# Turning every third job's probabilities by DMA instead of TensorE, and three low halves on GpSimd

## The chip, the cores and the metric

The kernel runs on one core of one Trainium2 chip. The metric is the device time of one execution in microseconds. Beside it stands one profiled execution, from which all rows below are taken.

## The reference, cut to what matters

Input x is (4, 1024, 1024) in fp32, the context the same. The output is `x1 + ffn(layernorm(x1))` with `x1 = x + attention(layernorm(x), ctx, ctx)`:

```python
q, k, v = ...            # 16 heads of 64; k = v = context
scores = jnp.einsum('bhqd,bhkd->bhqk', q, kj) * SCALE
scores = jnp.where(causal, -jnp.inf, scores)      # key index > query index
p = softmax(scores); out = jnp.einsum('bhqk,bhkd->bhqd', p, v)
...
soft = sigmoid(pweight) - sigmoid(nweight)        # (1024, 1024, 4 bits)
weight = jnp.einsum('oin,n->oi', soft, exps * sigmoid(mask_weight)) * scale[0]
return jnp.einsum('bsi,oi->bso', input, weight) + bias
```

## The kernel before, in words

**Tiles and jobs.** The 4 x 1024 rows are 32 tiles of 128 queries; tile t has i = t % 8 and sees i + 1 blocks of 128 keys. The 16 heads of a tile are worked off in jobs of 4, 4, 2, 2, 1, 1, 1, 1 heads for i = 0 to 7, so a tile has 4, 8 or 16 steps, one job each; j.q is the step's number within its tile, j.n its number in the whole (352 in all). Tiles with i of 4 to 7 (16 steps, one head per job, 5 to 8 blocks) are called long here.

**Precision.** Every operand of a matrix product is held as two f16 numbers, a high half (ScalarE rounds) and a low half (what is left, by a subtraction), side by side. Scores are two products per key block (`qt`, and `qs`, which is `qt` with its two 64-row halves swapped by DMA).

**One job's way.** `scores` (TensorE, L354, L355, mask L358) into one of two `slot` banks; `maxima` (VectorE, L554); `exponentials` (ScalarE, L451) into `p32`; `transpose_p` (TensorE, L367) turns each fp32 block of `p32` into `ptb`, in pieces of up to four blocks; `high_parts` (ScalarE, L461) and `low_parts` (VectorE, L561) split each piece out of `ptb` into `pt_hi` and `pt_lo`; `values` (TensorE, L381, L383) multiplies them with the context into `oacc`. `output` (ScalarE, L468) copies four heads' results out, `add_attention` (GpSimd, L743 to L752) adds them to the tile's row.

**Order.** Each engine's program is a loop over the jobs, written out by hand, with semaphores between the engines. TensorE's step for job j is:

```python
scores(JOBS[j.n + 2])
values(JOBS[j.n - 2])
transpose_p(j)
linear(k, m0, m1)        # a share of the linear layer of tile k = t - 3 (L399)
```

ScalarE's is `output` of the group that job j-2 closed, `high_parts(j)`, `exponentials(j+2)`, then at fixed steps the high half of y (`y_split`, L490), of a context tile (`c_split`, L483) or of the queries (`q_split`, L475). VectorE's is `maxima(j+2)`, `reciprocals`, `low_parts(j)`, then at fixed steps the low halves of the same three (L601, L596, L590), the moments for the layer norms (L575, L578), and `result` (L610), which adds the linear layer's bank `ffnb` to the row and frees that bank. GpSimd computes the layer norms (`deviation`, `normalise` L719), `add_attention` and `add_bias` (L737).

**The DMA queue of SyncE (SP)** works in order too: in step 0 of a tile it stores tile t-4 and swaps `qs` of tile t+1; in the middle it loads x and the context of tile t+3; after y's low half it turns y (L283); in the last step it turns the keys (L264) and the queries (L270) of tile t+2. The turns are `dma_start_transpose`, which transposes f16 blocks of 128x128 from SBUF to SBUF. The fixed steps stand in the tables Y_HI, Y_LO, C_HI, C_LO, Q_STEPS and BIAS. In the first 16 steps, tiles 0 to 3, the weights are built beside the attention.

Of the kernel before, what the change touches and what calls it, by code (L numbers as in the profile page):

```python
# [6 lines left out]
ALU = mybir.AluOpType  # L7
# [6 lines left out]
P = 128  # L14
# [29 lines left out]
class Job:  # L44


    def __init__(self, n, t, q, chunk0):
# [6 lines left out]
        blocks = self.heads * (self.i + 1)  # L54
        count = -(-blocks // 4)
        size = -(-blocks // count)
# [7 lines left out]
for _t in range(TILES):  # L64
    FIRST.append(len(JOBS))
    for _q in range(H // HPJ[_t % NT]):
        JOBS.append(Job(len(JOBS), _t, _q, JOBS[-1].chunks[-1][0] + 1 if JOBS else 0))
FIRST.append(len(JOBS))
LAST_OF_GROUP = [j.n for j in JOBS if j.closes_group]
# [46 lines left out]
Q_STEPS = {4: (0, 1, 2, 3), 8: (1, 2, 4, 6), 16: (3, 5, 8, 11)}  # L116
BIAS = {4: 2, 8: 4, 16: 9}
# [25 lines left out]

def reached(eng, s, value):
    if value > 0:
        eng.wait_ge(s, value)


def build(nc, x, ctx_in, pweight, nweight, exps, bexps, mask_weight, scale, pbias, nbias, biasscale, out):
# [6 lines left out]
    with ExitStack() as stack:  # L156
# [10 lines left out]
        spare32 = sb("spare32", [P, DM], F32)  # L167
# [4 lines left out]
        qs = sb("qs", [P, 2, H, P], F16)  # L172
        p32 = sb("p32", [P, 2, 8 * P], F32)
        pt_hi = sb("pt_hi", [P, 2, 8 * P], F16)
        pt_lo = sb("pt_lo", [P, 2, 8 * P], F16)
# [20 lines left out]
        def as_f32(m, place):  # L196
# [4 lines left out]
                 (ring[:, 6, :], spare32[:, :]), (as_f32(v16, 5), as_f32(yt, 0))]  # L201
# [22 lines left out]
        t_done, hi_done, lo_done, pv_done = sem("t_done"), sem("hi_done"), sem("lo_done"), sem("pv_done")  # L224
        osb_done, osb_added = sem("osb_done"), sem("osb_added")
# [15 lines left out]
        def _(sp):  # L241
# [30 lines left out]
            def swap_q(t):  # L272
                sp.wait_ge(q_in[t % 2], 16 * (t // 2 + 1))
                sp.dma_start(qs[0:D, t % 2], qt[D:P, t % 2]).then_inc(qs_in[t % 2], 16)
                sp.dma_start(qs[D:P, t % 2], qt[0:D, t % 2]).then_inc(qs_in[t % 2], 16)
# [20 lines left out]
            swap_q(0)  # L296
# [9 lines left out]
            for t in range(TILES):  # L306
                n = steps(t)
                for s in range(n):
                    if s == 0:
                        if t >= 4:  # L310
                            store(t - 4)
                        if t + 1 < TILES:
                            swap_q(t + 1)
# [11 lines left out]
                    if s == n - 1 and t + 2 < TILES:  # L325
                        turn_k(t + 2)
# [11 lines left out]
        def _(pe):  # L338
            def scores(j):
                i, t = j.i, j.t  # L340
                reached(pe, p_done, j.n - 1)
                if j.q == 0:
                    pe.wait_ge(qs_in[t % 2], 32 * (t // 2 + 1))
                    pe.wait_ge(k_in[t % 2], 16 * (t // 2 + 1))
                place0 = t - i
                for hh in range(j.heads):
                    h, base = j.head0 + hh, hh * HEAD_STRIDE[i]
                    first = 0
                    while first <= i:
# [5 lines left out]
                        last = pe.matmul(dst, qs[:, t % 2, h, :], keys, start=False, stop=end <= i,  # L355
# [6 lines left out]
            def transpose_p(j):  # L362
                pe.wait_ge(p_done, j.n + 1)
# [7 lines left out]
            def values(j):  # L371
                if j.opens_group:
                    reached(pe, osb_done, j.group)
                pe.wait_ge(lo_done, j.chunks[-1][0] + 1)
                for hh in range(j.heads):
                    h = j.head0 + hh
                    for blk in range(j.i + 1):
                        k = hh * (j.i + 1) + blk
                        cols = slice(k * P, (k + 1) * P)
                        v = v16[:, (j.t - j.i + blk) % V_PLACES, h]  # L380
                        pe.matmul(oacc[:, h % GROUP, :], pt_hi[:, j.par, cols], v,  # L381
                                  start=blk == 0, stop=False, skip_group_check=True)
                        last = pe.matmul(oacc[:, h % GROUP, 0:D], pt_lo[:, j.par, cols], v[:, 0:D],  # L383
# [62 lines left out]
        def _(act):  # L446
            def exponentials(j):
                act.wait_ge(mx_ready, j.n + 1)
                for hh in range(j.heads):
# [5 lines left out]
                last.then_inc(p_done, 1)  # L455

            def high_parts(j):
                reached(act, pv_done, j.n - 1)
                for c, blocks in j.chunks:
                    act.wait_ge(t_done, c + 1)  # L460
                    nc.scalar.activation(pt_hi[:, j.par, P * blocks.start:P * blocks.stop],  # L461
                                         ptb[:, c % 2, 0:P * len(blocks)], ACT.Copy, scale=P_SCALE
                                         ).then_inc(hi_done, 1)
# [86 lines left out]
        def _(dve):  # L550
# [6 lines left out]
            def low_parts(j):  # L557
                for c, blocks in j.chunks:
                    dve.wait_ge(hi_done, c + 1)
                    cols = slice(P * blocks.start, P * blocks.stop)  # L560
# [261 lines left out]
```

## Time and profile before

| | us |
|---|---|
| median of 3 runs | 1275.42 (1273.55 to 1277.51) |
| profiled execution, its own time | 1274.72 |
| its span, first to last instruction | 1272.9 |
| TensorE busy (matmul) | 1166.4 (92%) |
| VectorE busy | 1034.5 (81%) |
| ScalarE busy | 928.5 (73%) |
| GpSimd busy | 597.1 (47%) |
| DMA queue q1, share of 16 engines | 47.2% |

The span is what the engines' records cover; the execution's own time is 1.8 us longer. A busy TensorE is not one at its peak, since matmuls overlap: its pace is read from the start of one group to the start of the next, as the chain of waits gives it. A wait is idle time of one engine with the instruction that ended it.

### The profile page before, as it was taken

What the parts mean: (1) busy time and instruction counts of PE and PEld (TensorE: products, weight loads), DVE (VectorE), ACT (ScalarE), POOL (GpSimd) and SP (SyncE); (2) the same over time, 40 slices, a digit from 0 to 9 for tenths busy, and PEclk for the clock granted to TensorE, in tenths of its full rate; (3) what the DMA queues carried; (4) which work ended last, traced back from release to release, by engine and by line L of the source; (5) the groups of instructions that cost most, each with busy time, mean ns of one, the idle gap of its engine ahead of it and who ended that gap; (6) DMA issues with size and microseconds to landing.
All of it is one profiled execution on the core that took longest, in us unless ns stands there. A gap on an engine that the chain in (4) does not pass through costs nothing.

```text
span 1272.9 us, 29189 instructions
## 1 busy us (share of the span) xinstructions
PE 1166.4 (92%) x11376; PEld 883.3 (69%) x11376; DVE 1034.5 (81%) x1593; ACT 928.5 (73%) x2019; POOL 597.1 (47%) x717
## 2 busy tenths in 40 slices
PE   0677788999999999999999999999999999999998
PEld 0666675677777677777776677787786677777763
DVE  4576677888898888888897888888988888888872
ACT  2688876777877777787777777777787787777750
POOL 3399865433324954433325853333237844332241
PEclk9888899999999999999999999999999999999999
DMA  8979843543224955433316764444326755220112
GB/s 220 305 242 309 296 133 80 127 98 79 68 84 82 203 133 123 90 90 70 97 51 138 166 144 102 103 82 100 67 68 150 169 131 117 67 68 19 35 34 66
DMA packets 228984, 152.92 MB, mean 120 GB/s; under 512 B 204272, under 2 KB 204272, under 8 KB 228848
## 3 DMA queue, kind: packets, MB, share of 16 engines
q1 hardware_dynamic: 227264, 148.92, 47.2%
q8 instruction: 91, 1.49, 0.5%
q10 hardware_dynamic: 1584, 2.14, 0.5%
q14 instruction: 45, 0.37, 0.1%
HBM read 67.15 MB, written 16.78 MB: 66 GB/s over the span
## 4 chain that ended last, share of the span: by engine, by line
PE 63%; DVE 15%; POOL 6%; issue 5%; ACT 5%; DMA 4%; SPq 2%; ACTq 1%; POOLq 0%
PE ffnb L399 19%; PE ptb L367 15%; PE oacc L381 7%; PE slot L354 7%; PE slot L355 7%; DVE pt_lo L561 5%; PE oacc L383 4%; DVE stats L575 4%; POOL v L758 3%; ACT pt_hi L461 2%; DVE mx L554 2%; PE slot L358 2%; DVE ring L610 1%; ACT osb L468 1%; DMA yt<-in_L_ffn_nweight_dram 1%
## 5 line engine op out<-in xcount | busy, mean ns | idle before, releaser
L561 DVE SCALAR_TENSOR_TENSOR pt_lo<-ptb,pt_hi 128x384 f16<-128x384 f32 (+2 forms) x688 | 382.8, 597 | 119.7 <-ACT pt_hi L461 117.5
L461 ACT ACTIVATE pt_hi<-ptb 128x384 f16<-128x384 f32 (+2 forms) x688 | 326.4, 527 | 166.2 <-PE ptb L367 165.5
L451 ACT ACTIVATE p<-slot,mx 128x512 f32<-128x512 f32 (+7 forms) x512 | 378.5, 748 | 52.1 <-DVE mx L554 50.0
L399 PE MATMUL ffnb<-wt,yt 128*128 128x512 f16 x1464 | 371.0, 379 | 19.7 <-DVE ring L610 17.9
L554 DVE TENSOR_REDUCE mx<-slot 128x1 f32<-128x640 f32 (+7 forms) x352 | 359.4, 1021 | 21.3 <-PE slot L358 18.6
L367 PE MATMUL ptb<-id,p 128*128 128x128 f32 x2304 | 323.7, 279 | 11.1 <-DVE pt_lo L561 10.0
L354 PE MATMUL slot<-kt,qt 128*128 128x128 f16 (+3 forms) x1056 | 270.5, 286 | 32.6 <-DMA qs<-qt 28.0
L743 POOL TENSOR_TENSOR att<-osb 128x256 f32<-128x256 f32 x128 | 99.1, 774 | 421.9 <-ACT osb L468 397.7
L355 PE MATMUL slot<-kt,qs 128*128 128x128 f16 (+3 forms) x1056 | 270.0, 285 | 0.0
L367 PEld LDWEIGHTS ptb<-id,p 128*128 128x128 f32 x2304 | 246.3, 141 | 18.2 <-issue 15.7
L381 PE MATMUL oacc<-v,pt_hi 128*128 128x128 f16 x2304 | 244.2, 220 | 3.6 <-DVE pt_lo L561 1.9
L383 PE MATMUL oacc<-v,pt_lo 128*128 128x64 f16 x2304 | 234.7, 193 | 0.0
L399 PEld LDWEIGHTS ffnb<-wt,yt 128*128 128x128 f16 x1464 | 140.8, 98 | 124.8 <-issue 23.9
L381 PEld LDWEIGHTS oacc<-v,pt_hi 128*128 128x128 f16 x2304 | 205.6, 98 | 20.2 <-ACT osb L468 2.6
L383 PEld LDWEIGHTS oacc<-v,pt_lo 128*128 128x128 f16 x2304 | 200.8, 98 | 0.4
L354 PEld LDWEIGHTS slot<-kt,qt 128*128 128x128 f16 x1056 | 105.8, 100 | 94.7 <-issue 33.9
L355 PEld LDWEIGHTS slot<-kt,qs 128*128 128x128 f16 x1056 | 104.6, 99 | 58.1 <-issue 0.6
L468 ACT ACTIVATE osb<-oacc 128x512 f32<-128x512 f32 x128 | 76.6, 599 | 53.5 <-PE oacc L383 52.7
L358 PE MATMUL slot<-maskb,idb 128*128 128x128 bf16 x512 | 112.0, 223 | 0.0
L451 ACT ACTIVATION_READ_ACCUMULATOR p<-slot,mx 128x1 f32 x512 | 108.5, 212 | 0.0
L752 POOL TENSOR_TENSOR ring<-ring,att 128x256 f32<-128x256 f32 x128 | 99.9, 781 | 10.1
L746 POOL TENSOR_TENSOR att<-att,rinv 128x256 f32<-128x256 f32 x128 | 88.8, 694 | 11.3 <-DVE rinv L569 1.4
(78 smaller groups left out, 1064.6 us busy)
## 6 DMA issues: line engine op xcount, KB each, us to landing
ring<-in_x_dram SPq DMA_DIRECT2D x32, 512.0 KB, 4.9
cin<-in_ctx_dram SPq DMA_DIRECT2D x32, 512.0 KB, 4.0
qs<-qt SPq DMA_DIRECT2D x64, 256.0 KB, 3.9
out_dram<-ring SPq DMA_DIRECT2D x32, 512.0 KB, 2.9
v<-in_L_ffn_pweight_dram SPq DMA_DIRECT2D x20, 512.0 KB, 7.0
kt<-in_L_ffn_nweight_dram SPq DMA_DIRECT2D x15, 512.0 KB, 7.7
kt<-in_L_ffn_pweight_dram SPq DMA_DIRECT2D x5, 512.0 KB, 5.1
ring<-in_L_ffn_pweight_dram SPq DMA_DIRECT2D x5, 512.0 KB, 5.4
```

Source lines behind the costliest of these rows:

```text
L354: pe.matmul(dst, qt[:, t % 2, h, :], keys, start=True, stop=False, skip_group_check=True)
L355: last = pe.matmul(dst, qs[:, t % 2, h, :], keys, start=False, stop=end <= i, skip_group_check=True)
L358: last = pe.matmul(slot[:, j.par, base + i * P:base + (i + 1) * P], idb[:, :], maskb[:, :], start=False, stop=True, skip_group_check=True)
L367: last = pe.transpose(ptb[:, c % 2, at * P:(at + 1) * P], p32[:, j.par, k * P:(k + 1) * P], id32[:, :])
L381: pe.matmul(oacc[:, h % GROUP, :], pt_hi[:, j.par, cols], v, start=blk == 0, stop=False, skip_group_check=True)
L383: last = pe.matmul(oacc[:, h % GROUP, 0:D], pt_lo[:, j.par, cols], v[:, 0:D], start=False, stop=blk == j.i, skip_group_check=True)
L399: last = pe.matmul(dst, yt[:, k % 2, a * KT_N + kk, :], wt[:, c, kk, half * 512:half * 512 + 512], start=r == 0, stop=r == 3 * KT_N - 1)
L451: last = nc.scalar.activation(p32[:, j.par, hh * j.keys:(hh + 1) * j.keys], slot[:, j.par, base:base + j.keys], ACT.Exp, bias=mx[:, j.par, ...
L461: nc.scalar.activation(pt_hi[:, j.par, P * blocks.start:P * blocks.stop], ptb[:, c % 2, 0:P * len(blocks)], ACT.Copy, scale=P_SCALE).then_ ...
L554: nc.vector.tensor_reduce(mx[:, j.par, 0:j.heads], src[:, 0:j.heads, 0:j.keys], AX_X, ALU.max, negate=True).then_inc(mx_ready, 1)
L561: nc.vector.scalar_tensor_tensor(pt_lo[:, j.par, cols], ptb[:, c % 2, 0:P * len(blocks)], P_SCALE, pt_hi[:, j.par, cols], ALU.mult, ALU.su ...
L752: nc.gpsimd.tensor_tensor(dst, dst, att[:, :, :].rearrange("p h d -> p (h d)"), ALU.add).then_inc(x1_ready, 1)
```

## The change

In long tiles, jobs with q % 3 == 2 (q = 2, 5, 8, 11, 14) are "turned" jobs; j.d is their running number. Such a job has no pieces, so `transpose_p`, `high_parts` and `low_parts` do nothing for it. Instead ScalarE copies the whole of `p32` to the f16 high half in `p16` right behind its exponentials, VectorE computes the low half in `p16` in the step before the job's own, behind the maxima of the job after, SP turns both halves with one transposing DMA into `ptd`, and `values` reads them there. `p16` and `ptd` are single; `spare32`, whose place the weights used, is gone and `p16` serves for it. `pt_hi` and `pt_lo` become one array `pt`.

Besides: `qs` is single and is swapped in two halves of 8 heads at the steps of SWAP, each behind the scores of the same half of the tile before; the keys' turn of long tiles other than i = 7 moves from step 15 to step 9; the load of the context and the turn of y move one step later in long tiles; in tiles from 4 on with 8 or 16 steps GpSimd, not VectorE, computes the three low halves (y, context, queries); VectorE computes y's moments behind `result` and no longer ahead of it.

```diff
+        self.d = turned if self.heads == 1 and q % 3 == 2 else None
+        count = -(-blocks // 4) if self.d is None else 0
...
+SWAP = {4: (0, 2), 8: (2, 6), 16: (6, 14)}
...
+def turn_k_step(t):
+    return 9 if steps(t) == 16 and t % NT < NT - 1 else steps(t) - 1
+def low_on_pool(t):
+    return t > 3 and steps(t) > 4
...
+        p16 = sb("p16", [P, 2 * 8 * P], F16)
-        qs = sb("qs", [P, 2, H, P], F16)
+        qs = sb("qs", [P, H, P], F16)
+        pt = sb("pt", [P, 2, 2 * 8, P], F16)
+        ptd = sb("ptd", [P, 2 * 8, P], F16)
...
+            def turn_p(j):
+                sp.wait_ge(p16_lo, j.d + 1)
+                if j.d > 0:
+                    sp.wait_ge(pv_done, TURNED[j.d - 1].n + 1)
+                sp.dma_start_transpose(ptd[:, 0:2 * j.blocks], p16[:, 0:2 * j.keys]).then_inc(pt_in, 16)
...
+            def swap_q(t, half):
+                heads = slice(H // 2 * half, H // 2 * (half + 1))
                 sp.wait_ge(q_in[t % 2], 16 * (t // 2 + 1))
+                if t > 0:
+                    sp.wait_ge(s_done, FIRST[t - 1] + steps(t - 1) // 2 * (half + 1))
+                sp.dma_start(qs[0:D, heads], qt[D:P, t % 2, heads]).then_inc(qs_in[half], 16)
+                sp.dma_start(qs[D:P, heads], qt[0:D, t % 2, heads]).then_inc(qs_in[half], 16)
...
                 for s in range(n):
+                    if s + 1 < n and JOBS[FIRST[t] + s + 1].d is not None:
+                        turn_p(JOBS[FIRST[t] + s + 1])
+                    if t + 1 < TILES:
+                        if s == SWAP[n][0]:
+                            swap_q(t + 1, 0)
+                        if s == SWAP[n][1]:
+                            swap_q(t + 1, 1)
...
-                    if s == C_LO[n] and t + 3 < TILES:
+                    if s == C_LO[n] + n // 16 and t + 3 < TILES:
                         load_c(t + 3)
-                    for k in y_at(t, s, 2):
+                    for k in y_at(t, s - n // 16, 2):
                         if k != TILES - 2:
                             turn_y(k)
+                    if s == turn_k_step(t) and t + 2 < TILES:
+                        turn_k(t + 2)
...
             def values(j):
-                pe.wait_ge(lo_done, j.chunks[-1][0] + 1)
+                if j.d is None:
+                    pe.wait_ge(lo_done, j.chunks[-1][0] + 1)
+                else:
+                    pe.wait_ge(pt_in, 16 * (j.d + 1))
+                turned = pt[:, j.par] if j.d is None else ptd
...
             def exponentials(j):
                 act.wait_ge(mx_ready, j.n + 1)
+                if j.n > 1 and JOBS[j.n - 2].d is not None:
+                    act.wait_ge(p16_lo, JOBS[j.n - 2].d + 1)
...
+                if j.d is not None:
+                    act.wait_ge(p_done, j.n + 1)
+                    reached(act, pt_in, 16 * j.d)
+                    nc.scalar.activation(p16[:, 0:j.keys], p32[:, j.par, 0:j.keys], ACT.Copy, scale=P_SCALE
+                                         ).then_inc(p16_hi, 1)
...
+            def low_part_unturned(j):
+                dve.wait_ge(p16_hi, j.d + 1)
+                nc.vector.scalar_tensor_tensor(p16[:, j.keys:2 * j.keys], p32[:, j.par, 0:j.keys], P_SCALE,
+                                               p16[:, 0:j.keys], ALU.mult, ALU.subtract).then_inc(p16_lo, 1)
...
                     maxima(JOBS[j.n + 2])
+                if j.n + 1 < len(JOBS) and JOBS[j.n + 1].d is not None:
+                    low_part_unturned(JOBS[j.n + 1])
...
-                for k in y_at(t, s, 2):
-                    y_split(k)
-                if s == C_LO[steps(t)] and t + 2 < TILES:
-                    c_split(t + 2)
+                if not low_on_pool(t):
+                    for k in y_at(t, s, 2):
+                        y_split(k)
+                    if s == C_LO[steps(t)] and t + 2 < TILES:
+                        c_split(t + 2)
...
-                for k in y_begun(t, s):
-                    y_moments(k)
                 for k, m0, m1 in matmuls_at(t, s):
                     for half in range(2):
                         if m0 < MATMULS // 2 * (half + 1) <= m1:
                             result(k, half)
+                for k in y_begun(t, s):
+                    y_moments(k)
...
+            def y_split(k):                    # GpSimd; c_split and q_split alike
+                pool.wait_ge(y_hi, k + 1)
+                nc.gpsimd.tensor_tensor(y16[:, 1, :, :], norm32[:, :].rearrange("p (k c) -> p k c", c=P),
+                                        y16[:, 0, :, :], ALU.subtract).then_inc(y_lo, 1)
...
+                if low_on_pool(t):             # GpSimd, behind add_attention of the step
+                    for k in y_at(t, s, 2):
+                        y_split(k)
+                    if s == C_LO[steps(t)] and t + 2 < TILES:
+                        c_split(t + 2)
+                    if q_at(t, s, 3):
+                        q_split(t + 2)
```

## Rows read from the trace of the kernel before

**Rows 1.** The page: busy us, share, instructions; TensorE's granted clock in tenths, 40 slices.
```profile
PE 1166.4 (92%) x11376; PEld 883.3 (69%) x11376; DVE 1034.5 (81%) x1593; ACT 928.5 (73%) x2019; POOL 597.1 (47%) x717
...
PEclk9888899999999999999999999999999999999999
```

**Rows 2.** Windows, tiles 12 to 15: busy PE, PEld, DVE, ACT, POOL, clock, DMA share.
```profile
490.60:532.60 42.00, 40.13 (x441) 30.59 (x438) 35.42 (x65) 31.01 (x74) 17.06 (x24) 1.00 0.56 106
532.60:575.20 42.60, 41.30 (x443) 32.09 (x440) 37.25 (x63) 32.99 (x73) 16.10 (x22) 1.00 0.37 92
575.20:621.90 46.70, 45.74 (x491) 35.21 (x489) 41.53 (x63) 36.35 (x73) 16.20 (x22) 1.00 0.35 82
621.90:673.00 51.10, 50.48 (x548) 38.54 (x546) 46.38 (x64) 39.65 (x72) 15.04 (x22) 1.00 0.25 63
```

**Rows 3.** The chain of waits, tiles 12 to 15: start us, us, what.
```profile
521.42 0.58 PE ptb L367 x5
...
523.72 0.74 PE ptb L367 x5
...
560.25 0.69 PE ptb L367 x6
562.81 0.69 PE ptb L367 x6
...
605.23 0.80 PE ptb L367 x7
...
608.09 0.80 PE ptb L367 x7
...
644.89 0.91 PE ptb L367 x8
...
648.05 1.03 PE ptb L367 x8
```

**Rows 4.** Groups of instructions by line: count, busy us, mean ns, idle before.
```profile
L561 DVE SCALAR_TENSOR_TENSOR pt_lo<-ptb,pt_hi 128x512 f16<-128x512 f32 x304 | 198.8, 685 | 69.2 <-ACT pt_hi L461 67.5
L461 ACT ACTIVATE pt_hi<-ptb 128x512 f16<-128x512 f32 x304 | 169.5, 597 | 89.9 <-PE ptb L367 89.9
...
L737 POOL TENSOR_TENSOR ring<-ring,bias_row 128x1024 f32<-128x1024 f32 x32 | 75.3, 2353 | 0.1
...
L596 DVE TENSOR_TENSOR v<-cin,v 128x1024 f16<-128x1024 f32 x32 | 45.5, 1423 | 2.9 <-ACT v L483 2.9
...
L483 ACT CAST v<-cin 128x1024 f16<-128x1024 f32 x32 | 33.5, 1047 | 1.5 <-DMA cin<-in_ctx_dram 1.5
```

**Rows 5.** Waits between 206 and 1178 us: total us, times, longest.
```profile
PE ffnb L399 <- DVE ring L610: 16.3, 21, 1.2
...
PE ptb L367 <- DVE pt_lo L561: 7.2, 18, 2.0
```

**Rows 6.** Timeline of GpSimd and VectorE: start us, us, engine, line, instruction.
```profile
442.89 1.20 POOL L719 TENSOR_SCALAR norm<-ring,rstd 128x1024 f32<-128x1024 f32 x1
...
601.67 2.24 POOL L719 TENSOR_SCALAR norm<-ring,rstd 128x1024 f32<-128x1024 f32 x1
...
601.78 1.22 DVE L596 TENSOR_TENSOR v<-cin,v 128x1024 f16<-128x1024 f32 x1
```

**Rows 7.** DMA: one query turn alone, 1129 to 1135 us; then all key turns.
```profile
q1 hardware_dynamic: 2080, 0.52, 46.3%
...
qt<-q SPq DMA_TRANSPOSE x1, 4.3
...
kt<-v SPq DMA_TRANSPOSE x32, 6.5
```

**Rows 8.** Timeline of TensorE and VectorE around one job's scores, i = 6.
```profile
604.41 0.22 PE L358 MATMUL slot<-maskb,idb 128*128 128x128 bf16 x1
...
604.99 0.68 DVE L610 TENSOR_TENSOR ring<-ffnb,ring 128x512 f32<-128x512 f32 x1
605.59 1.08 DVE L554 TENSOR_REDUCE mx<-slot 128x1 f32<-128x896 f32 x1
```

More of the change, by code:

```diff
@@ L44, with __init__ @@
 class Job:
-    def __init__(self, n, t, q, chunk0):
+    def __init__(self, n, t, q, chunk0, turned):
         self.n, self.t, self.q = n, t, q
@@ L53, in __init__ @@
         self.par = n % 2
-        blocks = self.heads * (self.i + 1)
-        count = -(-blocks // 4)
-        size = -(-blocks // count)
+        self.blocks = blocks = self.heads * (self.i + 1)
+        self.d = turned if self.heads == 1 and q % 3 == 2 else None
+        count = -(-blocks // 4) if self.d is None else 0
+        size = -(-blocks // count) if count else 0
         self.chunks = [(chunk0 + c, range(size * c, min(size * c + size, blocks))) for c in range(count)]
@@ L66 @@
     for _q in range(H // HPJ[_t % NT]):
-        JOBS.append(Job(len(JOBS), _t, _q, JOBS[-1].chunks[-1][0] + 1 if JOBS else 0))
+        JOBS.append(Job(len(JOBS), _t, _q, sum(len(j.chunks) for j in JOBS), sum(j.d is not None for j in JOBS)))
 FIRST.append(len(JOBS))
+TURNED = [j for j in JOBS if j.d is not None]
 LAST_OF_GROUP = [j.n for j in JOBS if j.closes_group]
@@ L295, in _ @@
             turn_q(0)
-            swap_q(0)
+            swap_q(0, 0)
+            swap_q(0, 1)
             load_w(2)
@@ L341, in scores @@
                 reached(pe, p_done, j.n - 1)
+                if j.q in (0, steps(t) // 2):
+                    pe.wait_ge(qs_in[0 if j.q == 0 else 1], 32 * (t + 1))
                 if j.q == 0:
-                    pe.wait_ge(qs_in[t % 2], 32 * (t // 2 + 1))
                     pe.wait_ge(k_in[t % 2], 16 * (t // 2 + 1))
@@ L354, in scores @@
                         pe.matmul(dst, qt[:, t % 2, h, :], keys, start=True, stop=False, skip_group_check=True)
-                        last = pe.matmul(dst, qs[:, t % 2, h, :], keys, start=False, stop=end <= i,
+                        last = pe.matmul(dst, qs[:, h, :], keys, start=False, stop=end <= i,
                                          skip_group_check=True)
@@ L362, in transpose_p @@
             def transpose_p(j):
-                pe.wait_ge(p_done, j.n + 1)
+                if j.d is None:
+                    pe.wait_ge(p_done, j.n + 1)
                 for c, blocks in j.chunks:
@@ L378, in values @@
                         k = hh * (j.i + 1) + blk
-                        cols = slice(k * P, (k + 1) * P)
                         v = v16[:, (j.t - j.i + blk) % V_PLACES, h]
-                        pe.matmul(oacc[:, h % GROUP, :], pt_hi[:, j.par, cols], v,
+                        pe.matmul(oacc[:, h % GROUP, :], turned[:, k, :], v,
                                   start=blk == 0, stop=False, skip_group_check=True)
-                        last = pe.matmul(oacc[:, h % GROUP, 0:D], pt_lo[:, j.par, cols], v[:, 0:D],
+                        last = pe.matmul(oacc[:, h % GROUP, 0:D], turned[:, j.blocks + k, :], v[:, 0:D],
                                          start=False, stop=blk == j.i, skip_group_check=True)
@@ L460, in high_parts @@
                     act.wait_ge(t_done, c + 1)
-                    nc.scalar.activation(pt_hi[:, j.par, P * blocks.start:P * blocks.stop],
-                                         ptb[:, c % 2, 0:P * len(blocks)], ACT.Copy, scale=P_SCALE
-                                         ).then_inc(hi_done, 1)
+                    nc.scalar.activation(pt[:, j.par, blocks.start:blocks.stop, :],
+                                         ptb[:, c % 2, 0:P * len(blocks)].rearrange("p (k c) -> p k c", c=P),
+                                         ACT.Copy, scale=P_SCALE).then_inc(hi_done, 1)
             def output(g):
```

32 lines of the change are left out of this document (17 added, 15 removed).

## The prediction

> **What bounds the kernel now.** I read the page's busy times first, then the long tiles (16 steps, key tiles i = 4 to 7), then the chain of waits, and only then the helpers' waits. TensorE is busy 1166.4 of 1272.9 us, VectorE 1034.5, ScalarE 928.5, and TensorE's clock stands at its full level (2.4 GHz) in nearly every slice [rows 1]. The four long tiles of one batch last 42.0, 42.6, 46.7 and 51.1 us, and VectorE is busy for 35.4, 37.3, 41.5 and 46.4 us of them, ScalarE for 31.0, 33.0, 36.4 and 39.7 [rows 2]. Nothing is idle by much; the question is who has slack.
>
> The chain answers it. In the last long tile it runs through TensorE alone: eight transposes of probabilities 0.91 us, and the same point one job later is 3.16 us on. With seven, six and five blocks the transposes take 0.80, 0.69 and 0.58 us and a step at full pace 2.86, 2.56 and 2.30 us [rows 3]. Sixteen such steps are 50.6, 45.8, 41.0 and 36.8 us: against the measured 51.1, 46.7, 42.6 and 42.0 the i = 7 tile is bound by TensorE to 1%, the i = 4 tile loses 5.2 us to its helpers, and the four together lose 8.2 us. So a TensorE instruction taken out of a long tile is worth nearly its full duration, provided that the helpers can follow the faster pace.
>
> **The change, part by part.**
>
> *Transposes removed.* Jobs with q = 2, 5, 8, 11, 14 of the 16 long tiles: 80 jobs. Each batch saves 5 x (0.58 + 0.69 + 0.80 + 0.91) = 14.9 us of TensorE, four batches 59.6 us, all of it on the path [rows 3]. I take -60. At worst it is worth half where the helpers set the pace (i = 4 and 5: 5 x 1.27 x 4 = 25 us at risk).
>
> *ScalarE and VectorE work of such a job.* Before: two or three pieces, for seven or eight blocks two of up to 0.60 us (ScalarE) and 0.69 us (VectorE) [rows 4]. After: one instruction over up to 1024 elements from SBUF. The nearest rows are the two halves of a whole context tile, 128x1024 from SBUF: 1.05 us on ScalarE, and on VectorE 1.42 in the mean [rows 4] and 1.22 in a single one [rows 6]. So nothing is gained or lost: within -0.2 and +0.3 us per job, taken as 0. What moves is the place: VectorE does the low half one step early, behind the maximum, so that step carries maximum + turned half + the ordinary low parts, 3.3 us for seven blocks against a TensorE step of 2.86, and the next carries only the maximum. The low parts of job d-1 thereby come 1.1 us later, but their reader, the value products, stands two steps on.
>
> *Three low halves per tile to GpSimd.* From tile 4 on in tiles of 8 and 16 steps VectorE loses three instructions of 1.4 us; GpSimd's nearest two-input instruction of that size takes 2.35 us [rows 4], so it gains 7 us per tile where it is busy 15 to 17 of 42 to 51 us [rows 2]. VectorE's load falls by 4.2 us a tile, to 31, 33, 37 and 42 us, against TensorE's new full pace of 36.8 - 2.9 = 33.9, then 37.5, 41.8 and 46.0. That leaves it 8 to 12% of slack, as much relatively as it has today at i = 5 to 7. ScalarE is unchanged at 31, 33, 36.4, 39.7: 9 to 14%. TensorE's waits for VectorE between 206 and 1178 us are 16.3 us for the bank of the linear layer and 7.2 us for low parts [rows 5]; the result now stands ahead of the moments. I take back less than half, -11; bounds 0 and -25.
>
> The Trainium skill (GPSIMD Engine Reference, Key points) warns that GpSimd shares its SBUF interfaces with VectorE when a VectorE instruction has two SBUF inputs, and the new low half is one. The trace agrees in kind: a GpSimd normalisation takes 1.20 us alone and 2.24 us with such a VectorE subtraction of 1.22 us beside it [rows 6]. In that row GpSimd paid and not VectorE; by the rule 80 collisions of 1.0 us would land on GpSimd, which has the room, and the sum stays.
>
> *Transposing transfers and their landing.* SP issues one per such job. A full one (16 blocks of 128x128) takes 46.3% of 6 us = 2.8 us of all 16 DMA engines and lands 4.3 us after its issue in a quiet stretch; the one for the keys, issued behind two loads, has a median of 6.5 us [rows 7]. With 10 to 16 blocks I estimate 3.3 to 4.3 us quiet. All 80 add 80 x 6.5/8 x 2.8 = 182 us, 14% of share, where the long tiles use 25 to 56% [rows 2].
>
> Is it in time? For i = 6, counted from the start of scores(d+1) in step d-1: scores 1.0, VectorE's lateness (0 to 1.0: in one row the scores end near 604.6, a result of 0.68 us goes first, and the maximum starts at 605.59 [rows 8]), maximum 1.08, low half 1.1, landing 3.95: 7.1 to 8.1 us. TensorE wants it in step d+2 behind its scores: 2.86 + 2.06 + 2.86 + 0.8 = 8.6 us. For i = 7 the same count gives a slack of 0.7 to 1.7 us, for i = 4 and 5 of 0.1 to 1.1. A quiet transfer is hidden, barely; one that meets loads, a stored tile or the keys' turn comes about 2.2 us later (6.5 against 4.3) and stalls TensorE 1 to 1.5 us. I count one of the five jobs per tile: 16 x 1.3 = +20 us. Bounds: 0, and 80 x 1.5 = +120 if all were like the keys' turn.
>
> *Waits added, and what stands behind them.* SP waits for the low half, and behind it stand the swap halves, loads and turns of the coming steps, none due within a tile. ScalarE's copy waits for the landing of the turned job before (three jobs back), and high parts and exponentials of later jobs stand behind it; that landing falls some 0.3 to 1.3 us ahead of the copy in the same count, so a late transfer can hold ScalarE too. The next exponential of the same parity waits for the low half, long done by then. The moments of y come one result (0.68 us) later, and ScalarE's copy of y waits in order for them. Together +7; bounds 0 and +25.
>
> *At nothing:* the swap in halves and the single buffer of swapped queries (second half issued in step 14, needed at the earliest in the first step of the next tile, two steps and some 6 us later), the keys' turn moved from step 15 to 9 (nobody waits for it), the start up to 206 us (no turned job, same loads) and the last 45 us.
>
> **Sum.** -60 - 11 + 20 + 7 = -44 us on the profiled execution's 1274.72 us: 1230.7. That execution lies 0.7 us under the median of 1275.42, so on the runs' scale 1231 us.
>
> **Rivals.**
> - *All of it arrives.* Transfers hide and the helpers keep up: -60 - 20 = 1195 to 1210. For it: the quiet landing fits. Against: today's i = 4 tile, where VectorE has 4% of slack to the full pace, already loses 14%, and the new balance is 8 to 12% everywhere. Chance 0.12.
> - *The helpers set the pace.* ScalarE with 9% of slack and VectorE's uneven steps (3.3 us, then 1.1) eat half: each batch gains 5 us instead of 11, 1255. For it: in the i = 4 to 6 tiles the engines' loads lie within 10% of each other. Chance 0.20.
> - *Slower: the turned probabilities arrive late as a rule.* Place: the value products of each turned job. If the landing is 6.5 us on average, as for the keys' turn, each waits some 1.2 us longer than now counted: 1231 - 20 + 96 = 1307. It decides from a mean stall of 0.9 us per turned job ((60 + 11) / 80), that is from a landing of about 5.7 us. Against: the turns of queries and y land in 4.3. Chance 0.12. The Trainium skill (VectorE: DVE Perf Modes, The three transpose paths) gives 390 ns for a 128x128 block on TensorE and 1309 ns through DMA; 13 blocks one after another would be 17 us a job by it, but the trace has 16 blocks landed in 4.3 us, and TensorE's at 0.11 us each, so only the direction of that rule holds here.
> - *It doesn't do what it says*, for instance the transfers are serialised with the loads so that SP falls behind whole steps: in the chance above.
>
> **How the numbers follow.** Forecast (1215 to 1248) 0.56, all arrives 0.12, helpers 0.20, slower 0.12. A measurement tells 0.3%, 4 us, from no change. Faster: 0.56 + 0.12 + 0.17 of the helpers' case = 0.85; same 0.04; slower 0.11. The range takes in most of the first two rivals: 1205 to 1264.
>
> **What would show it.** Transposes of probabilities down by 520 to 1784. The i = 7 tile at 47 to 48 us, the i = 4 tile near 38. TensorE's waits for the landing of turned probabilities: about 20 us in total, in few jobs, worst where a load stands ahead. VectorE's waits for ScalarE smaller, its busy time down by some 85 us, GpSimd's up by 150. The prediction is wrong if the landing has a median over 5.5 us, if TensorE waits for it in most turned jobs, or if ScalarE's copy waits for the previous landing as a rule; then the gain goes to nothing or below.

## The result, and the profile after

The changed kernel takes 1263.35 us in the median (1260.02 to 1265.73) against 1275.34: a ratio of 0.9903, 95% interval 0.9876 to 0.9931. It is 12 us faster where 44 were forecast. The profiled execution took 1262.99 us, its span is 1261.1.

The work that was to go has gone. The page's busy line, with the shares of the span:

```profile
PE 1117.8 (89%) x10856; PEld 822.3 (65%) x10856; DVE 983.8 (78%) x1450; ACT 922.9 (73%) x1939; POOL 744.5 (59%) x780
```

Against [rows 1] TensorE has 520 matmuls fewer, VectorE is 51 us less busy (85 were forecast) and GpSimd 147 us more. But the long tiles 12 to 15, windows with the same columns as [rows 2]:

```profile
484.10:524.70 40.60, 37.91 (x422) 28.20 (x419) 31.77 (x58) 31.50 (x71) 25.76 (x28) 1.00 0.57 126
524.70:568.10 43.40, 39.20 (x423) 29.02 (x420) 36.59 (x56) 32.53 (x68) 22.97 (x25) 1.00 0.63 130
568.10:614.10 46.00, 42.81 (x456) 31.14 (x454) 39.67 (x56) 35.91 (x68) 23.44 (x25) 1.00 0.60 130
614.10:665.80 51.70, 47.73 (x503) 35.33 (x502) 44.86 (x57) 39.87 (x68) 22.95 (x25) 0.97 0.51 112
```

They last 181.7 us together, where before they lasted 182.4, though TensorE's full pace fell from 174.2 to 159.2. So 22.5 us are now lost, where there were 8.2. The i = 7 tile was forecast at 47 to 48 us and the i = 4 tile near 38; they last 51.7 and 40.6.

Most of the gain doesn't lie in the long tiles at all. Counted from one tile's first masking product (L358, now L391) to the next one's, the profiled execution is 5.6 us shorter ahead of tile 4, where no turned job runs, 2.2 us in the short tiles of the later batches, and only 3.8 us in the sixteen long tiles (729.9 to 726.0 us). The forecast had put the first two at nothing. What made them shorter was not tried.

What was to be read first is the price of the new instruction, in the groups by line (x80 is all of them):

```profile
L611 DVE SCALAR_TENSOR_TENSOR p<-p 128x640 f16<-128x640 f32 (+3 forms) x80 | 110.3, 1378 | 16.1 <-ACT p L498 13.7
```

And one of them in the timeline of tile 15, with GpSimd's and TensorE's rows around it:

```profile
640.66 1.22 DVE L598 TENSOR_REDUCE mx<-slot 128x1 f32<-128x1024 f32 x1
640.67 1.20 POOL L771 TENSOR_SCALAR norm<-ring,rstd 128x1024 f32<-128x1024 f32 x1
...
641.83 2.13 POOL L794 TENSOR_TENSOR v<-cin,v 128x1024 f16<-128x1024 f32 x1
...
642.13 2.91 DVE L611 SCALAR_TENSOR_TENSOR p<-p 128x1024 f16<-128x1024 f32 x1 [0.25 <-ACT p L498]
...
646.16 0.67 DVE L659 TENSOR_TENSOR ring<-ffnb,ring 128x512 f32<-128x512 f32 x1
...
646.89 0.82 PE L436 MATMUL ffnb<-wt,yt 128*128 128x512 f16 x3 [2.81 <-DVE ring L659]
```

GpSimd's subtraction runs from 641.83 to 643.96. The turned low half, begun at 642.13, ends at 645.04, 1.08 us after GpSimd: it waited for nearly all that was left of the GpSimd instruction and then did its work. I call this a meeting. Behind it stand two low parts and the result, and TensorE waits 2.81 us for the bank. The maximum beside GpSimd's normalisation, which reads PSUM, kept its 1.22 us. A turned low half that meets nothing takes 0.82, 0.95, 1.09 or 1.22 us by its size, 1.02 in the mean. VectorE thus pays 110.3 - 80 x 1.02 = 29 us more, at its fullest steps. All of it falls on 24 of the 80, job 8 and job 11 in twelve long tiles each: 18.5 us behind the bias addition (always job 11), 5.2 behind a normalisation and 4.8 behind the context's new low half (both job 8). The low halves of y and of the queries hold none of them.

The long wait has a second price. TensorE's granted clock fell to half, its 1.2 GHz level, 1.3 us after it (the row is a window, with the columns of [rows 2]):

```profile
648.20:651.60 3.40, 3.40 (x27) 3.12 (x26) 1.31 (x2) 3.00 (x5) 0.71 (x1) 0.50 1.00 323
```

The step that holds most of this stretch took 4.62 us from its masking product to the next one's, where such a step takes 3.16. There are two more such stretches of 3.4 us: at 672.1, just behind a wait of 2.1 us for the swapped queries, and at 924.7, at the end of one of 2.8 us for the bank. My estimate is 1.5 us each, some 4.5 us in all.

The waits between 206 and 1178 us, as in [rows 5]:

```profile
PE ffnb L436 <- DVE ring L659: 18.2, 14, 2.8
...
PE oacc L418 <- ACT osb L512: 12.7, 25, 1.6
...
PE oacc L418 <- DMA ptd<-p: 10.8, 9, 3.4
PE oacc L418 <- DVE pt L604: 7.6, 8, 1.2
...
PE slot L387 <- DMA qs<-qt: 5.7, 3, 2.2
```

And the transfers, as in [rows 7]:

```profile
ptd<-p SPq DMA_TRANSPOSE x80, 4.0
...
kt<-v SPq DMA_TRANSPOSE x32, 6.6
```

The transfers kept to the forecast: 4.0 us in the median, and TensorE waited for them 9 times.

### The profile page after: what moved, and what is told of

Read it like the earlier page. It is cut to its first block and busy times, and to the rows that moved or that the text cites. A ratio compares the mean times of both kernels' runs of the same rounds, so it can differ in the third digit from the quotient of the medians.

```text
span 1261.1 us, 28304 instructions
## 1 busy us (share of the span) xinstructions
PE 1117.8 (89%) x10856; PEld 822.3 (65%) x10856; DVE 983.8 (78%) x1450; ACT 922.9 (73%) x1939; POOL 744.5 (59%) x780
## 5 line engine op out<-in xcount | busy, mean ns | idle before, releaser
L436 PE MATMUL ffnb<-wt,yt 128*128 128x512 f16 x1464 | 374.1, 382 | 22.5 <-DVE ring L659 21.2
L604 DVE SCALAR_TENSOR_TENSOR pt<-ptb,pt 128x512 f16<-128x512 f32 (+2 forms) x528 | 295.4, 599 | 113.2 <-ACT pt L505 112.8
L505 ACT ACTIVATE pt<-ptb 128x512 f16<-128x512 f32 (+2 forms) x528 | 251.8, 529 | 63.9 <-PE ptb L401 62.7
L811 POOL TENSOR_TENSOR att<-osb 128x256 f32<-128x256 f32 x128 | 107.3, 838 | 296.7 <-ACT osb L512 269.3
L401 PE MATMUL ptb<-id,p 128*128 128x128 f32 x1784 | 251.3, 279 | 7.6 <-DVE pt L604 7.4
L418 PE MATMUL oacc<-v,pt 128*128 128x128 f16 x1784 | 189.2, 220 | 22.8 <-ACT osb L512 13.4
L401 PEld LDWEIGHTS ptb<-id,p 128*128 128x128 f32 x1784 | 191.8, 141 | 11.2 <-issue 9.8
L418 PEld LDWEIGHTS oacc<-v,pt 128*128 128x128 f16 x1784 | 158.1, 98 | 43.2 <-ACT osb L512 21.4
L420 PE MATMUL oacc<-v,pt 128*128 128x64 f16 x1784 | 181.5, 193 | 0.0
L420 PEld LDWEIGHTS oacc<-v,pt 128*128 128x128 f16 x1784 | 155.4, 98 | 0.0
L611 DVE SCALAR_TENSOR_TENSOR p<-p 128x640 f16<-128x640 f32 (+3 forms) x80 | 110.3, 1378 | 16.1 <-ACT p L498 13.7
L391 PE MATMUL slot<-maskb,idb 128*128 128x128 bf16 x512 | 111.7, 222 | 0.0
```

The lines of the kernel that those rows point to most:

```text
L391: last = pe.matmul(slot[:, j.par, base + i * P:base + (i + 1) * P], idb[:, :], maskb[:, :], start=False, stop=True, skip_group_check=True)
L401: last = pe.transpose(ptb[:, c % 2, at * P:(at + 1) * P], p32[:, j.par, k * P:(k + 1) * P], id32[:, :])
L418: pe.matmul(oacc[:, h % GROUP, :], turned[:, k, :], v, start=blk == 0, stop=False, skip_group_check=True)
L420: last = pe.matmul(oacc[:, h % GROUP, 0:D], turned[:, j.blocks + k, :], v[:, 0:D], start=False, stop=blk == j.i, skip_group_check=True)
L436: last = pe.matmul(dst, yt[:, k % 2, a * KT_N + kk, :], wt[:, c, kk, half * 512:half * 512 + 512], start=r == 0, stop=r == 3 * KT_N - 1)
L505: nc.scalar.activation(pt[:, j.par, blocks.start:blocks.stop, :], ptb[:, c % 2, 0:P * len(blocks)].rearrange("p (k c) -> p k c", c=P), ACT ...
```

## The experiments

All times are medians; the kernel before ran beside each group on the same chip (1272.6 to 1275.8 us), and the ratios, with their 95% intervals, are against it. "Kept clear" is e3, from which most later ones are built. "Held" is what the 80 turned low halves take, in sum, above the shortest of their size: 29.2 us in the changed kernel.

**Part by part, and the meeting taken away**

*e1_halves_back*: `low_on_pool` always False.

> The changed kernel with one part undone: the three low halves per tile are VectorE's again, all else as changed. Port theory (the turned jobs' low half reads two SBUF operands, and such a VectorE instruction and a GpSimd tensor_tensor exclude each other; jobs 8 and 11 of each long tile met the context's and the queries' low half on GpSimd and took up to 2.9 us instead of 1.0 to 1.2): those two encounters go, the bias addition's may stay, VectorE's load rises 4.2 us per long tile; in all 1250 to 1258 us. Order theory (the loss is VectorE's uneven steps and ScalarE's later exponentials, whoever does the halves): a fuller VectorE is worse, 1266 to 1275 us.

Measured: 1269.29 us, ratio 0.9958 [0.9941, 0.9974]. The order theory's number. But its trace has the meeting still, at job 11, with the bias addition, a GpSimd instruction that was there before the change. VectorE is held for 21 us, against 29. The 6 us under the kernel before are not in the long tiles, which are 2.1 us longer than before in its profiled execution: as it stands, turning by DMA alone gained nothing there.

*e2_halves_alone*: the kernel before, with the three halves on GpSimd.

> The kernel before with only the three low halves moved to GpSimd (tiles from 4 on with 8 or 16 steps), no turned jobs, VectorE's order as before. Port theory: VectorE has then almost no instruction with two SBUF operands left, so nothing is met and the lighter VectorE gives 8 to 12 us: 1264 to 1267 us. Order theory: the same lighter VectorE, the same 8 to 12 us; both fail if it is slower than 1275, which would mean that GpSimd's own lateness costs.

Measured: 1267.41 us, ratio 0.9946 [0.9928, 0.9964], 8 us faster, the lower end of what both theories gave.

*e3_clear_of_it*: kept clear.

```diff
-BIAS = {4: 2, 8: 4, 16: 9}
+BIAS = {4: 2, 8: 4, 16: 6}
...
+                        if steps(t) == 16:
+                            pool.wait_ge(p16_lo, JOBS[FIRST[t] + 8].d + 1)
                         c_split(t + 2)
...
+                        if steps(t) == 16:
+                            pool.wait_ge(p16_lo, JOBS[FIRST[t] + 11].d + 1)
                         q_split(t + 2)
```

> The changed kernel with GpSimd's long instructions kept clear of the turned low halves in the long tiles: the context's half waits until the low half of job 8 is done, the queries' until that of job 11, and the bias addition moves from step 9 to step 6, behind the context's half. The same work on every engine. Port theory: the turned low half falls from a mean of 1.38 us to about 1.03, VectorE's late results (2.8 and 1.4 us waits of TensorE) go, 20 to 30 us less than the changed kernel's 1263: 1233 to 1243 us. Order theory: no difference from 1263 beyond 4 us.

Measured: 1240.21 us, ratio 0.9729 [0.9710, 0.9749]. The same work on each engine, two waits more and one instruction earlier: 23 us less than the changed kernel. The order theory falls. Nearly all of it, 20 us, is in the long tiles, and the granted clock no longer falls in them, which by the estimate above is some 4.5 of the 23 us. Its turned low halves (minimum/median/maximum, ns) and its tiles 12 to 15:

```profile
L611 DVE SCALAR_TENSOR_TENSOR p<-p x80: 815/1092/1828, 217.0 to 1194.5; 128x640 f16<-128x640 f32 x20, 128x768 f16<-128x768 f32 x20, 128x896 f16<-128x896 f32 x20, 128x1024 f16<-128x1024 f32 x20
```

```profile
479.20:520.70 41.50, 37.96 (x422) 28.27 (x420) 31.82 (x59) 31.56 (x71) 25.62 (x28) 1.00 0.58 124
520.70:562.10 41.40, 38.35 (x419) 28.90 (x417) 34.78 (x56) 32.45 (x66) 21.55 (x25) 1.00 0.66 136
562.10:606.90 44.80, 42.45 (x460) 31.46 (x458) 38.09 (x56) 35.97 (x68) 21.90 (x25) 1.00 0.63 133
606.90:655.70 48.80, 46.58 (x507) 34.09 (x503) 42.18 (x56) 39.34 (x68) 22.03 (x25) 1.00 0.55 119
```

The largest duration falls from 2.9 to 1.8 us, the time held from 29.2 to 6.4 us (what is left is job 8 behind a normalisation), and the four tiles to 176.5 us.

*e4_halves_out*: GpSimd's three instructions cut to 8 elements, `v[:, 0:1, D:D + 8]` and the like (the context's from tile 10 on).

> The changed kernel with GpSimd's three low halves cut to 8 elements each (left out: the low halves of y, of the queries, and of the context from tile 10 on). Port theory: like keeping clear, 1233 to 1243 us, with only the bias addition still met. Order theory: at most 4 us below 1263.

Measured: 1259.26 us, ratio 0.9872 [0.9849, 0.9896]. A miss: removing the halves brings 4 us, where moving them and the bias addition brought 23. The timeline says why:

```profile
561.14 2.36 POOL L809 TENSOR_TENSOR ring<-ring,bias_row 128x1024 f32<-128x1024 f32 x1
...
561.43 2.88 DVE L611 SCALAR_TENSOR_TENSOR p<-p 128x768 f16<-128x768 f32 x1 [0.25 <-ACT p L498]
```

The bias addition alone holds job 11's low half for 1.9 us, and in sum 26.5 us are still held. The theory stands, but what it named, the new halves, was the smaller part of it.

**Which edit carries it**

*e5_bias_early*: the changed kernel with `BIAS` 16: 6 alone.

> The changed kernel with only the bias addition moved from step 9 to step 6 of long tiles; no wait added. Port theory in its first form (the three new halves are what the turned low half meets): nothing of the gain, 1263. Port theory in its second form (any long GpSimd tensor_tensor counts, the bias addition as much as the halves; what decides is when GpSimd runs): the context's half and now the bias addition stand where job 8 is done, and the queries' half slides forward to where job 11 is, so about the changed kernel's time again, 1255 to 1265 us, far from the 1240 of the kernel that is kept clear.

Measured: 1260.47 us, ratio 0.9892 [0.9876, 0.9907]: the changed kernel's time, as the second form had it. The queries' half slid into the place of the bias addition and now holds job 11; 25.2 us are held.

*e9_waits_only*: the two waits alone.

> The changed kernel with only the two waits (the context's half behind the low half of job 8, the queries' behind that of job 11), the bias addition left in step 9. Timing form of the port theory: job 8 is clear, job 11 still meets the bias addition, so TensorE's wait after job 8 shrinks and the one after job 11 stays: 1248 to 1256 us, between the changed kernel (1263) and the one kept clear (1240); together with the bias addition moved alone (1260) the two edits give more than their sum. If the waits alone carry it: 1240 to 1244.

Measured: 1257.82 us, ratio 0.9875 [0.9850, 0.9900], 5.5 us less. Alone the edits give 3 and 5.5 us, neither clear of the two intervals, together 23. The time held explains it: each alone leaves one meeting per long tile standing, 25.2 us in sum either way, and only both leave 6.4. In e9's timeline job 8's low half meets a normalisation, one tensor input only, and job 11's the bias addition:

```profile
550.99 1.20 POOL L771 TENSOR_SCALAR norm<-ring,rstd 128x1024 f32<-128x1024 f32 x1
...
551.16 1.83 DVE L611 SCALAR_TENSOR_TENSOR p<-p 128x768 f16<-128x768 f32 x1
...
560.15 2.35 POOL L805 TENSOR_TENSOR ring<-ring,bias_row 128x1024 f32<-128x1024 f32 x1
...
560.44 2.88 DVE L611 SCALAR_TENSOR_TENSOR p<-p 128x768 f16<-128x768 f32 x1 [0.25 <-ACT p L498]
```

*e6_one_operand*:

```diff
-nc.vector.scalar_tensor_tensor(p16[..., j.keys:2 * j.keys], p32[...], P_SCALE, p16[..., 0:j.keys], ALU.mult, ALU.subtract)
+nc.vector.tensor_scalar(p16[..., j.keys:2 * j.keys], p32[...], P_SCALE, None, ALU.mult)
```

> The changed kernel with the turned low half as a scaling of the fp32 probabilities alone, one SBUF operand in place of two (left out: the subtraction of the high half). Port theory in the form 'two SBUF operands': every one of the 80 has nearly one duration per shape, none over 1.4 us, and the time falls to 1232 to 1243 us. If VectorE and GpSimd exclude each other for any SBUF operand: still durations of 1.8 to 2.9 us at jobs 8 and 11, and 1255 to 1263 us.

Measured: 1245.09 us, ratio 0.9766 [0.9743, 0.9790]. Neither form as written. The scaling takes 0.56 us alone and is held just the same:

```profile
555.86 2.36 POOL L804 TENSOR_TENSOR ring<-ring,bias_row 128x1024 f32<-128x1024 f32 x1
...
556.14 2.48 DVE L611 TENSOR_SCALAR p<-p 128x768 f16<-128x768 f32 x1 [0.25 <-ACT p L498]
...
564.05 0.56 DVE L611 TENSOR_SCALAR p<-p 128x768 f16<-128x768 f32 x1 [0.25 <-ACT p L498]
```

So two operands aren't needed for it: 27.9 us are held, as before. The 80 instructions take 74.5 us in place of 110.3, and that is where the 18 us come from, as far as the rows show. But one SBUF operand isn't enough either. VectorE's moments read one fp32 operand from SBUF, and in the kernel before 33 of the 128 ran beside a GpSimd instruction of over 0.5 us that had begun at least 0.15 us earlier; not one took over 0.70 us:

```profile
L575 DVE BATCH_NORM_STATS2 stats<-ring x128: 669/679/695, 7.0 to 1240.4; 128x6 f32<-128x512 f32 x128
```

So it depends on the instruction. The Trainium skill (GPSIMD Engine Reference, Key points) names both cases, two SBUF inputs and a two-port mode; a duration of 0.56 us for 768 columns, against 0.95 with two operands, fits a mode of the second kind, which no run here shows by itself.

**Order and landing**

*e7_behind_low_parts*: kept clear, with `low_part_unturned` behind `low_parts(j)`.

> The kernel kept clear (1240) with VectorE's turned low half behind the ordinary low parts of its step, not ahead of them. Order theory: what is left of the loss is the ordinary low parts that come late, so 5 to 15 us faster, 1225 to 1235. Landing theory: the turned probabilities start about 1.1 us later against a slack of 0.1 to 1.7 us, TensorE's waits for their landing rise from 9 us to 20 or 30, and the time to 1245 to 1260 us.

Measured: 1297.27 us, ratio 1.0174 [1.0145, 1.0202], slower than the kernel before. TensorE's waits for the landing:

```profile
PEld oacc L418 <- DMA ptd<-p: 55.7, 53, 2.9
PE oacc L418 <- DMA ptd<-p: 43.8, 51, 2.8
```

9.4 us in 7 waits became 43.8 in 51. The direction was the landing theory's, the size far beyond it: 44 us of waits where it gave 20 or 30, and 57 us more time where it gave 5 to 20. The transfer starts 1.1 us later and TensorE stalls in most turned jobs. ScalarE's copy now waits 16.4 us for landings, where it waited 7.3, and GpSimd's halves wait longer too; that these make the rest is not shown.

*e8_shifted*: kept clear, turned jobs at q = 3, 6, 9, 12, 15, swaps ahead of the turn.

> The kernel kept clear with the turned jobs at q = 3, 6, 9, 12, 15 instead of 2, 5, 8, 11, 14, so that VectorE's turned low half no longer shares step 7 with the result of the first half of the linear layer, and ScalarE's copy not step 0 with y's high half; GpSimd's halves wait for jobs 3, 6 and 12, and the swaps of the queries stand ahead of the turn in SP's order. If what is left are these crowded steps (TensorE waits 0.6 to 1.4 us for the bank at step 8 of each long tile, and 0.5 to 0.9 us twice near its start for ScalarE, and 1.4 to 2.1 us for the swapped queries at a batch's end): 10 to 18 us less than 1240, 1222 to 1230. If the loss is spread over all steps: within 4 us of 1240.

Measured: 1243.55 us, ratio 0.9746 [0.9728, 0.9765]. No gain. The bias addition now met job 9's low half (2.89 and 2.35 us in tiles 14 and 15), 16.3 us were held in place of 6.4, and the waits for the landing rose to 14.6 us. Inconclusive on crowding, since it changed what meets what.

**What is left at 1240 us**

*e10_step8_empty*: kept clear, with

```diff
+SHARES = [3, 3, 3, 3, 3, 3, 3, 3, 0, 4, 3, 4, 3, 3, 4, 3]
+        if n == 16 and t > 4:
+            out.append((k, sum(SHARES[:s]), sum(SHARES[:s + 1])))
```

> The kernel kept clear with the linear layer's shares of matmuls per step 3,3,3,3,3,3,3,3,0,4,3,4,3,3,4,3 instead of 16 times 3 (tiles from 5 on), so that TensorE does not ask for the bank in step 8 while VectorE still has the turned low half and two low parts ahead of the result. If those waits (1.0 to 1.4 us in each long tile) are on the path: 10 to 18 us less than 1240, 1222 to 1230. If they only take up slack that another queue gives back (a shorter step 8 makes the helpers late): within 5 us of 1240.

Measured: 1243.99 us, ratio 0.9756 [0.9733, 0.9779]. TensorE's waits for the bank, 13.5 us, are gone. Its waits for low parts rose from 5.7 to 10.7 us, and those for ScalarE from 19.2 to 25.7.

*e11_y_later*: kept clear, `Y_HI` 16: 2, `Y_LO` 16: 3, and GpSimd's half behind job 5's low half.

> The kernel kept clear with ScalarE's high half of y in step 2 of long tiles instead of step 0, where the turned job's copy stands too, and GpSimd's low half of y in step 3 behind the low half of job 5. If ScalarE's crowded step 0 is what makes TensorE wait at each long tile's start (0.3 to 0.9 us twice or three times): 8 to 16 us less, 1224 to 1232. Otherwise within 5 us of 1240.

Measured: 1239.62 us, ratio 0.9727 [0.9704, 0.9750]. No difference.

*e12_both*: both edits.

> The kernel kept clear with both edits: the linear layer's step 8 empty and y's halves later. If both crowded steps are on the path: 1212 to 1222 us. If the stalls are handed from one queue to the next: 1232 to 1242.

Measured: 1237.72 us, ratio 0.9707 [0.9685, 0.9729], in the range of the second: stalls are handed on.

Then each piece of a turned job that is not TensorE's was cut to one block from tile 8 on: ScalarE's copy (e13), VectorE's low half (e14), the transfer (e15), all three (e16), for example

```diff
+                cut = j.keys if j.t < 8 else P
-                nc.vector.scalar_tensor_tensor(p16[:, j.keys:2 * j.keys], p32[:, j.par, 0:j.keys], ...
+                nc.vector.scalar_tensor_tensor(p16[:, j.keys:j.keys + cut], p32[:, j.par, 0:cut], ...
```

> The kernel kept clear (1240) with ScalarE's copy of a turned job cut to one block of 128 columns from tile 8 on (left out: the other 4 to 7 blocks, 60 jobs, some 0.6 us of ScalarE each). If ScalarE's queue holds the rest: 10 to 16 us less. If it is VectorE's queue: at most 5 less, from the low half that can start earlier. If the landing: 3 to 8 less.

Measured: 1234.23 us, ratio 0.9696 [0.9666, 0.9726].

> The kernel kept clear with VectorE's turned low half cut to one block from tile 8 on (left out: the other blocks, 60 jobs, some 0.7 us of VectorE each, and the transfer starts that much earlier). If VectorE's crowded steps hold the rest: 15 to 25 us less than 1240, 1215 to 1225. If ScalarE's queue: at most 5 less.

Measured: 1229.97 us, ratio 0.9663 [0.9644, 0.9682].

> The kernel kept clear with the transposing transfer cut to 2 blocks of 128x128 from tile 8 on (left out: the other 8 to 14 blocks; landing some 1.5 to 2 us earlier, engines' time gone). TensorE's own waits for it are 9.4 us in total in that kernel, so 5 to 10 us less if only these count, none if they are handed on, and more than 12 only if the transfers also delay the others.

Measured: 1236.39 us, ratio 0.9710 [0.9687, 0.9733].

> The kernel kept clear with all three cut. If the turned jobs' own side work holds the remaining 17 us per batch: three batches at up to 12 us each, 1205 to 1215 us. If 1228 or more, the rest lies in the ordinary work, which a shorter TensorE step no longer covers.

Measured: 1220.77 us, ratio 0.9593 [0.9575, 0.9611]. Its tiles 12 to 15:

```profile
481.20:521.40 40.20, 37.93 (x422) 28.23 (x420) 29.50 (x59) 29.62 (x71) 24.76 (x28) 1.00 0.47 103
521.40:561.20 39.80, 38.07 (x413) 28.63 (x411) 30.73 (x55) 30.34 (x67) 21.51 (x25) 1.00 0.45 102
561.20:604.70 43.50, 42.27 (x457) 31.29 (x454) 34.68 (x56) 33.30 (x68) 21.58 (x25) 1.00 0.40 94
604.70:651.30 46.60, 46.02 (x508) 34.09 (x506) 37.99 (x56) 36.01 (x67) 21.34 (x25) 1.00 0.33 76
```

6, 10 and 4 us, and 19 together: no single piece holds the rest, and none of the four fell in the range of the queue that it was to test. VectorE's low half is the largest. The sum lies between the two ranges of e16. 170.1 us against 176.5 with the pieces and 159.2 at full pace: per batch 6.4 us of stalls belong to the turned jobs' side work and 10.9 us remain with hardly any of it. Before, at a slower pace, 8.2 were lost.

*e17_no_last_turn*: both edits of e12, and `(q < 14 or self.i < NT - 1)` added to the choice of turned jobs.

> The kernel with both crowded steps eased (1238) and job 14 of the i = 7 tiles turned by TensorE again (76 turned jobs, not 80), so that the swap of the queries' second half has no turn ahead of it at the batch's end. If that wait (5.2 us in three batches) is on the path: 3 x 2.2 less, 4 x 0.9 more for the transposes, so 1233 to 1237 us. If it is taken up elsewhere: 1238 to 1242.

Measured: 1236.74 us, ratio 0.9691 [0.9673, 0.9708]. Within the first range, but only 1 us from e12: TensorE's wait for the swap (5.2 us) is gone, and its waits for the landing rose from 12.6 to 16.5 us. It is the fastest version here that leaves nothing out, 27 us under the changed kernel and 39 under the one before.

## Why the prediction was wrong, point by point

The direction was right, the size not: -44 forecast, -12 measured. Even the direction owes something to luck, since 8 of the 12 us lie where the forecast had nothing.

**Transposes removed (-60): right as TensorE's pace.** Where nothing meets, the interval from one job to the next in tile 15 is 3.16, 2.25, 3.16 us as computed. With most meetings gone (e3) the sixteen long tiles are 24.0 us shorter than before, where the forecast, its terms for waits included, had 44 in all. It was "worth nearly its full duration, provided that the helpers can follow", and that condition failed.

**The step that failed** is "In that row GpSimd paid and not VectorE; by the rule 80 collisions of 1.0 us would land on GpSimd, which has the room, and the sum stays", and with it the new low half priced at 0 "within -0.2 and +0.3 us per job". In [rows 6] VectorE's instruction was the one that got through and GpSimd's normalisation the one that was stretched, and I took that for a rule. The trace of the kernel before already spoke against it. One tile later the same two instructions meet again, the normalisation 0.38 us ahead, and VectorE pays:

```profile
650.23 1.20 POOL L719 TENSOR_SCALAR norm<-ring,rstd 128x1024 f32<-128x1024 f32 x1
...
650.61 1.89 DVE L596 TENSOR_TENSOR v<-cin,v 128x1024 f16<-128x1024 f32 x1
```

So the 1.42 us in the mean of [rows 4] against the 1.22 of one were themselves VectorE's share: 25 of the 96 low halves of before took over 1.3 us, the longest 2.76. Who pays is who begins later, by a margin. In [rows 6] the normalisation is recorded as beginning 0.11 us ahead and still lost; under 0.17 us the rows show either outcome. From 0.17 us on, VectorE pays whenever over a quarter of a us is left of GpSimd's instruction. In the changed kernel 24 low halves begin after a long GpSimd instruction, and are held for what is left of it. The mean excess is 0.36 us, but it is 0.2 to 1.9 us in those 24 and nothing in the others, in steps that I had myself counted as full (3.3 us against 2.86). Taking most of the meetings away without touching the work gives 23 of the missing 32 us (e3), the clock's share included. That I looked only at the three moved halves and not at the bias addition, which stood unchanged in the path of the new instruction, is the same slip once more: e4 and e1 show it to be the larger part.

**Halves to GpSimd (-11): about right.** Alone they give -8 (e2). In the changed kernel they give -6 (against e1), though the context's half makes three of the 24 meetings.

**Landing (+20): half, and the mechanism right.** 4.0 us in the median, and 10.8 us of waits in 9 jobs. That the slack was 1 us is confirmed the hard way: 1.1 us later costs 57 us (e7). The slower rival didn't come about in the changed kernel, but e7 made it so: its place and its sign were right.

**Waits added (+7), and things priced at nothing.** ScalarE's copy waited 7.1 us for the landing of the job before, and TensorE 12.7 us for ScalarE's output, where it had waited 1.4. The swap of the queries' second half, "needed at the earliest in the first step of the next tile", costs TensorE 5.7 us in three batches, since it stands behind the last turned job on SP. Taking that job away moved the time by 1 us (e17), so it is not shown to be on the path.

**The rivals.** The time lies nearest to "The helpers set the pace" (1255), given 0.20. Its reason, loads too near to each other, may account for the rest but not for most: with the meetings thinned out the time is 1240, and there five easings of single queues (e10, e11, e13, e14, e15) gave -10 to +4. That kernel still loses 17 us per batch at 8 to 12% of slack, where the one before lost 8; I took nothing for the rise beyond the terms. How the 10.9 us per batch that e16 leaves are shared among ScalarE's output, the bank and the scores' buffers was not tried.

**The range** (1205 to 1264) took in most of the helpers' rival. That the measured time lies just inside it is luck: the meeting, by which it came out there, was not among the reasons for it.

## What to carry to other kernels

Before an instruction on SBUF operands is added to VectorE, list every long GpSimd instruction that can run at that moment, the old ones first: VectorE may be held for the whole rest of it, and that belongs in the sum as a stall at that step, not as a mean. It is cheap to cure: two waits that start GpSimd's long work right behind the VectorE instruction, and the bias addition moved three steps earlier, gave 23 us here with no work removed. Whose instruction is stretched is not read from one meeting: compare the minimum and the maximum of that line's durations in the trace you have. And work taken from a bottleneck engine whose helpers have only 8 to 12% of slack was worth less than half of its duration, even with the meetings thinned out. Last, look where a gain lies before you put it down to the change: here two thirds of it lay outside the tiles that the change was for.

## What the runs showed of the hardware

- VectorE instructions with two tensor operands in SBUF and GpSimd's exclude each other: a VectorE instruction of 0.95 us took 2.88 when a GpSimd addition of 2.36 us had begun 0.29 us before it, and 1.83 us behind a GpSimd scaling of 1.20 us, which has one tensor operand. GpSimd can be the one that is stretched, too (1.20 to 2.24 us in [rows 6]).
- The hold is regular. In twelve traces 387 low halves on VectorE (those of e6 among them) began at least 0.17 us after a GpSimd instruction of over 0.5 us, with over 0.2 us of it left; 385 took longer by what was left of it less 0.13 us (0.12 to 0.15), the other two, both in e12, kept their duration. Starts nearer to each other went either way.
- It holds for a VectorE scaling with one tensor operand, too (0.56 to 2.48 us in e6), but not for the moments, which also read one operand from SBUF (0.67 to 0.70 us in all 128). VectorE's maxima and low parts, which read PSUM, kept their durations beside GpSimd (1.22 us in the timeline above).
- After a wait of TensorE of 2.8 us the granted clock stood at its 1.2 GHz level for 3.4 us (0.50 in the window above), and one step took 4.62 us in place of 3.16. With the meetings thinned out (e3) it stayed at the full level from 230 to 1230 us.
- A transposing transfer from SBUF to SBUF of 10 to 16 blocks lands 3.4 to 4.3 us after its issue in the median by size, single ones up to 6.1, and 80 more of them left the other turns' landing nearly unchanged (keys 6.5 and 6.6 us in the median, queries 4.4 and 4.5, y 4.3 and 4.3).
